# A gated cross-attention and mixture-of-experts layer: bias as one matmul step, half-tile input load, one pair in the prologue, norm root on GpSimd, new step lists

## The reference, cut to what matters

```python
# x (8, 512, 256), ctx (8, 512, 128); 16 heads of 64; 8 experts, top 2
def xattn(q, kv):                       # per batch
    qh, kh, vh = heads(q @ Wq), heads(kv @ Wk), heads(kv @ Wv)
    attn = softmax(qh @ kh.T * 64 ** -0.5)
    return merge(attn @ vh) @ Wo + bo
def ffn(x):
    probs = softmax(x @ gate_w.T)
    comb = one_hot_weights(top_k(probs, 2))          # (tokens, 8)
    return sum(comb[:, e:e+1] * (x @ expert_w[e].T + expert_b[e]) for e in range(8))
x = x + tanh(g_xattn) * xattn(layernorm(x), ctx)
x = x + tanh(g_ffn) * ffn(layernorm(x))
```

## Time and profile before

| | |
|---|---|
| median of 3 runs | 1139.79 us (1138.34 to 1140.05) |
| profiled execution | 1140.45 us, span of its instructions 1138.6 us |
| mean granted TensorE clock | 0.975 |
| TensorE matmul busy | 1056.2 us (93%) |
| VectorE | 881.0 us (77%) |
| ScalarE | 812.9 us (71%) |
| GpSimd | 602.7 us (53%) |

### The profile page before, as it was taken

One profiled execution on the slowest core, in us unless ns is written; L12 is line 12 of the kernel. 1 busy time (PEld: TensorE's weight loads), 2 busy tenths in 40 slices (PEclk: granted clock), 3 DMA queues, 4 the chain that ended last, 5 costly groups with the idle time before them and its releaser, 6 DMA issues.

```text
span 1138.6 us, 29422 instructions
## 1 busy us (share of the span) xinstructions
PE 1056.2 (93%) x10784; PEld 786.4 (69%) x10784; DVE 881.0 (77%) x1559; ACT 812.9 (71%) x1403; POOL 602.7 (53%) x323
## 2 busy tenths in 40 slices
PE   8877898999989999899898999899998999999878
PEld 7555676677667776677676777667776777667676
DVE  7786688877887779877588778877788777887537
ACT  4878887678867698586695878667895768858500
POOL 2655665464645656465464756446565555647400
PEclk9889999999999999999899999999998999999999
DMA  3996968496685876676766868739676678669610
GB/s 126 192 181 131 175 150 143 90 177 129 135 134 116 158 155 123 123 148 120 136 135 127 159 121 168 140 84 177 131 135 140 117 140 158 125 109 162 123 33 18
DMA packets 554209, 152.09 MB, mean 134 GB/s; under 512 B 541896, under 2 KB 551504, under 8 KB 554064
## 3 DMA queue, kind: packets, MB, share of 16 engines
q1 hardware_dynamic: 554064, 150.16, 67.8%
HBM read 11.68 MB, written 4.19 MB: 14 GB/s over the span
## 4 chain that ended last, share of the span: by engine, by line
PE 64%; issue 12%; DVE 9%; POOL 8%; ACT 4%; DMA 2%; SPq 1%; DVEq 0%; POOLq 0%; ACTq 0%
PE MB L963 32%; PE ST L1070 14%; PE PV L1086 10%; POOL p_s L488 7%; PE MB L973 3%; PE ST L1095 2%; DMA pt_s<-p_s 2%; ACT pf L628 1%; PE ST L963 1%; PE MB L1043 1%; DVE p L925 1%; DVE nmax L787 1%; DVE ve L688 1%; DVE w L903 1%; DVE stats L676 1%
## 5 line engine op out<-in xcount | busy, mean ns | idle before, releaser
L488 POOL TENSOR_TENSOR p_s<-pf,p_s 128x1024 f16<-128x1024 f32 x256 | 549.7, 2147 | 456.9 <-ACT p_s L637 456.2
L787 DVE TENSOR_REDUCE nmax<-ST 128x2 f32<-128x1024 f32 x256 | 311.3, 1218 | 70.0 <-PE ST L1070 66.0
L628 ACT ACTIVATE pf<-ST,shifts 128x512 f32<-128x512 f32 x512 | 323.3, 686 | 3.2
L1086 PEld LDWEIGHTS PV<-v_s,pt_s 128*128 128x128 f16 x6144 | 206.3, 98 | 111.9 <-issue 71.5
L637 ACT ACTIVATE p_s<-pf 128x1024 f16<-128x1024 f32 x256 | 270.6, 1057 | 7.2
L1086 PE MATMUL PV<-v_s,pt_s 128*128 128x65 f16 x6144 | 233.1, 195 | 43.2 <-DVE o_n L803 35.5
L963 PE MATMUL MB<-ex_s,x2t_s 128*128 128x512 f32 x708 | 201.8, 422 | 0.0
L619 ACT ACTIVATE shifts<-nmax 128x2 f32<-128x2 f32 x256 | 51.7, 202 | 162.7 <-DVE nmax L787 162.0
L750 DVE SCALAR_TENSOR_TENSOR acc<-MB,comb,acc 128x256 f32<-128x256 f32 x236 | 114.1, 484 | 61.5 <-PE MB L963 56.7
L963 PEld LDWEIGHTS MB<-ex_s,x2t_s 128*128 128x128 f32 x708 | 129.6, 196 | 40.8 <-issue 16.5
L1070 PE MATMUL ST<-KH,QH 64*128 64x512 f32 x512 | 129.5, 502 | 19.5 <-ACT pf L628 12.2
(11 more groups left out here) (120 smaller groups left out, 1119.9 us busy)
## 6 DMA issues: line engine op xcount, KB each, us to landing
pt_s<-p_s SPq DMA_TRANSPOSE x512, 2.8
xin<-x SPq DMA_DIRECT2D x8, 512.0 KB, 4.7
out<-acc SPq DMA_DIRECT2D x8, 512.0 KB, 4.5
kvin<-kv_t SPq DMA_DIRECT2D x8, 256.0 KB, 4.2
acc<-expert_t SPq DMA_DIRECT2D x4, 256.0 KB, 3.9
xn<-expert_t SPq DMA_DIRECT2D x4, 256.0 KB, 4.3
pf<-wq SPq DMA_DIRECT2D x1, 768.0 KB, 7.1
pt_s<-wk SPq DMA_DIRECT2D x1, 512.0 KB, 5.7
```

The source lines that it names most:

```text
L488: pool.tensor_tensor(p_s[:, u, 1, :, :], pf[:, u % 2, :, :], p_s[:, u, 0, :, :], ALU.subtract).then_inc(p_lo, 1)
L628: last = act.activation(pf[:, u % 2, i, :], ST[u % 2][:, i, :], ACT.Exp, bias=shifts[:, u % 2, i:i + 1], scale=SCALE)
L787: dve.tensor_reduce(nmax[:, t % 2, :], ST[t % 2][:, :, :], AX.X, ALU.max, negate=True)\
L1086: last = pe.matmul(PV[:, col:col + HEAD + 1], pt_s[:, slot, a, i, k, :], v_s[:, c, k, (2 * p + i) % HEADS, :], start=(k == 0 and n == 0), ...
```

## The change

One diff with these edits:

- The bias of the experts: expert_b stands three times in a 72-row operand (`eb_s`: high part in rows 0 to 7 and 64 to 71, low part in 32 to 39, the rest zero), comb in 72 columns (high part at 0 and 32, low at 64), and each bias job becomes two fp32r matmuls of 256 columns. comb is written by one instruction, its copy into two places and its low part by two more; the gates job transposes 72 columns.
- x of batch 0 is loaded in two halves, and its sums start with the first.
- The prologue does q and k of one pair; q1, k1 and the bound come behind the first score tile of the first batch (PRO_JOBS).
- var + eps, the power, mean times it and its negative are four GpSimd instructions; lines 687 and 688 are gone. In the prologue GpSimd holds its own work back until xn is written; there and in the epilogue TensorE transposes each tile of xn as it comes.
- The logits are reduced and shifted straight from the bank; route part 0 is gone.
- The output of the last batch is stored in four DMAs, one for each tile.
- p_s has three slots, used as a ring, instead of four. Values stand six units back instead of five.
- The dummies ahead of ("x2t", 0) in the epilogue are put ahead of whichever x2t job comes first (NEXT_X2T); in the new order that is x2t0.
- Late weights use other rows and slots.
- All four step lists are replaced.

```diff
-PE_ORDER = (
...
+PE_ORDER = (
+    "scores", "scores values v2,0 v0,0 v1,0", "scores values v3,0", "scores values ot6 values", "scores k2 k3 values",
+    "scores values q2 ot7", "scores values", "scores values v3,1 wo3,0 v0,1", "scores values", "scores wo3,1 q3",
+    "scores values", "scores v2,1 ot0 values", "scores values q4 values x2t0 x2t1 k4", "scores values router v1,1",
+    "scores values logits k5 values", "scores ot1 k6 values", "scores values q6 wo0,1", "scores values",
+    "scores values q5 wo0,0", "scores values", "scores values q7 k7 expert0,0",
+    "scores values expert0,1 ot3 expert0,2 ot2 expert0,3 values", "scores",
+    "scores values expert1,0 bound wo1,1 expert1,1", "scores expert1,2 gates expert1,3 wo1,0 values",
+    "scores expert2,0 xt1 expert2,1 values", "scores values expert2,2 xt0",
+    "scores values expert2,3 ot4 expert3,0 bias0 values", "scores",
+    "scores bias1 expert3,1 ot5 q0 expert3,2 k0 wo2,1 q1 k1", "scores", "scores values expert3,3 wo2,0 values",
+)
-ACT_ORDER = (
...
+ACT_ORDER = (
+    "shift exp hi copy", "shift hi exp hi", "shift copy exp hi hi", "shift copy exp hi copy", "shift hi exp",
+    "shift copy exp hi copy hi", "shift exp hi copy", "shift exp hi copy", "shift exp", "shift copy exp hi copy",
+    "shift exp hi copy norm2 hi", "shift", "shift hi exp hi hi copy exp hi", "shift copy hi exp logits hi copy",
...
-DVE_ORDER = (
-    "maximum normalise take take", "maximum take take", "maximum normalise take", "maximum take normalise",
-    "maximum take take", "maximum take take take take sums2", "maximum moments2 take normalise", "maximum",
-    "maximum take take normalise bound", "maximum take normalise take take take take", "maximum take take normalise",
-    "maximum take route0 take route1", "maximum route2 take route3 take route4 take route5 normalise route6 take",
...
+DVE_ORDER = (
+    "maximum", "maximum take", "maximum normalise take take", "maximum take normalise take", "maximum take",
+    "maximum normalise", "maximum take take take normalise", "maximum take take", "maximum take",
+    "maximum take sums2", "maximum moments2 normalise take", "maximum take", "maximum normalise take take take take",
+    "maximum normalise take take sums1 take take", "maximum normalise route1 take", "maximum take moments1",
+    "maximum route2 take normalise route3", "maximum take", "maximum normalise route4 take take",
+    "maximum route5 take route6", "maximum normalise bound take take take", "maximum take take take take normalise",
...
-VALUES_BACK, SHIFT_BACK, EXP_BACK, COPY_BACK = 5, 0, 0, 0
+VALUES_BACK, SHIFT_BACK, EXP_BACK, COPY_BACK = 6, 0, 0, 0
-PF_SLOTS, P_SLOTS, PT_SLOTS = 2, TT, 6
+PF_SLOTS, P_SLOTS, PT_SLOTS = 2, 3, 6
-LATE_SLOTS, LATE_HI_AT, LATE_LO_AT = 4, 3, 4
+LATE_AT = list(range(10)) + [13, 14]
+LATE_SLOT = [0, 1, 2, 3, 0, 1, 2, 3, 0, 1, 0, 1]
+LATE_IN_XN = 8
+PRO_JOBS = 4
+NEXT_X2T = [name for name in LAST_JOBS if name[0] == "x2t"][0]
+BUSY_EPI = {("ot", PAIRS - 1): 3, ("wo", ROUNDS - 1, 0): 6, NEXT_X2T: 24, ("router",): 5, ("logits",): 3}
...
-            sp.dma_start(xin[:, :, :], x_v[:, 0:TT, :]).then_inc(x_in, 16)
+            sp.dma_start(xin[:, 0:2, :], x_v[:, 0:2, :]).then_inc(x_half, 16)
+            sp.dma_start(xin[:, 2:TT, :], x_v[:, 2:TT, :]).then_inc(x_in, 16)
...
+            sp.wait_ge(const_pool, 1)
+            for row0 in (0, 32, 64):
+                sp.dma_start(eb[row0:row0 + EXPERTS, :], expert_b).then_inc(small_in, 16)
...
+            for t in range(TT):
+                sp.wait_ge(job_free, epi.last_done(JOBS, ("bias", t // 2), ("expert", t, EC - 1)) + BANKS)
+                sp.dma_start(out_v[:, (BATCHES - 1) * TT + t:(BATCHES - 1) * TT + t + 1, :],
+                             acc[:, t:t + 1, :]).then_inc(y_out, 16)
...
+            pool.memset(eb[:, :], 0.0).then_inc(const_pool, 1)
             pool.memset(ident[:, :], 0.0).then_inc(const_pool, 1)
+            pool.memset(comb_w[:, :, :], 0.0).then_inc(const_pool, 1)
...
                 pool.wait_ge(var, n)
+                pool.tensor_tensor(ve[:, :], mv[:, :, 1], eps[:, :], ALU.add).then_inc(rstd_done, 1)
+                pool.wait_ge(rstd_done, 3 * n - 2)
                 pool.tensor_tensor(rstd[:, :], ve[:, :], minus_half[:, :], ALU.pow).then_inc(rstd_done, 1)
-                pool.wait_ge(rstd_done, n)
-                pool.tensor_tensor(shift[:, :], less[:, :], rstd[:, :], ALU.mult).then_inc(shift_done, 1)
+                pool.wait_ge(rstd_done, 3 * n - 1)
+                pool.tensor_tensor(shift[:, :], mv[:, :, 0], rstd[:, :], ALU.mult).then_inc(rstd_done, 1)
+                pool.wait_ge(rstd_done, 3 * n)
+                pool.tensor_tensor(shift[:, :], zero[:, :], shift[:, :], ALU.subtract).then_inc(shift_done, 1)
 
             power(1, ln1_var, ln1_rstd, ln1_shift)
+            pool.wait_ge(ln1_done, 1)
...
-                if it.kind != FIRST or p > 0:
-                    act.wait_ge(hi_turned[u], 16 * pair_count(it.b, p - 1))
-                act.activation(p_s[:, u, 0, :, :], pf[:, u % 2, :, :], ACT.Copy).then_inc(p_hi, 1)
+                before = divmod(p * TT + u - P_SLOTS, TT)
+                if it.kind != FIRST or before[0] >= 0:
+                    act.wait_ge(hi_turned[before[1]], 16 * pair_count(it.b, before[0]))
+                act.activation(p_s[:, it.ring(p, u, P_SLOTS), 0, :, :], pf[:, u % 2, :, :], ACT.Copy).then_inc(p_hi, 1)
...
-                    last = dve.tensor_copy(m1[:, :, :], m[:, 0:TT * EXPERTS].rearrange("p (t e) -> p t e", t=TT))
+                    raw = m[:, 0:TT * EXPERTS].rearrange("p (t e) -> p t e", t=TT)
+                    dve.tensor_reduce(less[:, :], raw, AX.X, ALU.max, negate=True).then_inc(lg_max, 1)
+                    dve.wait_ge(lg_max, it.b)
+                    last = dve.tensor_tensor(logit[:, :, :], raw, over(less), ALU.add)
...
-                    dve.tensor_scalar(comb[:, :, :], m2[:, :, :], tg[:, 1:2], None, ALU.mult).then_inc(comb_ready, 1)
+                    then(dve.tensor_scalar(comb[:, :, :], m2[:, :, :], tg[:, 1:2], None, ALU.mult))
+                    twice = comb_w[:, :, 0:64].rearrange("p t (a e) -> p t a e", a=2)[:, :, :, 0:EXPERTS]
+                    then(dve.tensor_copy(twice.bitcast(F32R),
+                                         comb[:, :, :].unsqueeze(2).broadcast_to([P, TT, 2, EXPERTS])))
+                    dve.tensor_tensor(comb_w[:, :, 64:WIDE].bitcast(F32R), comb[:, :, :], comb_w[:, :, 0:EXPERTS],
+                                      ALU.subtract).then_inc(comb_ready, 1)
...
+                    dve.tensor_tensor(eb_s[32:32 + EXPERTS, :], eb[32:32 + EXPERTS, :],
+                                      eb_s[32:32 + EXPERTS, :].bitcast(F32), ALU.subtract).then_inc(const_dve, 1)
...
-                        last = pe.matmul(m[:, DIM * i:DIM * (i + 1)], comb_t[:, tile(2 * name[1] + i)],
-                                         eb[:, :], start=True, stop=True)
+                        last = pe.matmul(m[:, DIM * i:DIM * (i + 1)], gates_t[:, tile(2 * name[1] + i)],
+                                         eb_s[:, :], start=True, stop=True)
```

More of the change, by code:

```diff
@@ L65 @@
 PE_ORDER = (
[L66 to L71, removed]
@@ L98 @@
+    "maximum take take take take take", "maximum take", "maximum take take take normalise",
 )
 POOL_ORDER = (
-    "low", "low", "low", "low", "low residual", "low power2", "low", "low", "low", "low", "low", "low", "low",
-    "low power1", "low", "low", "low", "low", "low", "low", "low", "low", "low", "low", "low", "low", "low",
-    "low context", "low", "low", "low", "low",
+    "low", "low", "low", "low", "low", "low", "low", "low", "low power2", "low residual", "low", "low", "low", "low",
@@ L320, in build @@
         small_in = sem("small_in")
-        late_in = [sem(f"late_in{n}") for n in range(LATE_SLOTS)]
+        late_in = [sem(f"late_in{n}") for n in range(4)]
         w_hi, wq_lo, w_lo = sem("w_hi"), sem("wq_lo"), sem("w_lo")
@@ L599, in row @@
                             exponential(b, *divmod(at, TT))
+                        if kind == FIRST and at == 0:
+                            for name in HI[PRO][PRO_JOBS:]:
+                                take_hi(pro, name)
                     elif part == "copy":
@@ L854, in row @@
                             maximum(b, *divmod(at, TT))
+                        if kind == FIRST and at == 0:
+                            for name in JOBS[PRO][PRO_JOBS:]:
+                                take_first(name)
                     elif part == "normalise":
@@ L910, in first @@
                     then(dve.tensor_tensor(mask[:, :, :], w1[:, :, :], over(r1), ALU.is_equal))
-                if part == 0:
-                    dve.wait_ge(job_free, it.done(JOBS, ("logits",)) + BANKS)
-                    then(dve.tensor_reduce(r1[:, :], m1[:, :, :], AX.X, ALU.max, negate=True))
-                    dve.tensor_tensor(logit[:, :, :], m1[:, :, :], over(r1), ALU.add).then_inc(lg_shift, 1)
-                elif part == 1:
```

(14 more changed lines are left out.)

188 lines of the change are left out of this document (98 added, 90 removed).

## The result

| | before | after |
|---|---|---|
| median, same chip | 1139.07 us (4 runs, 1134.05 to 1140.05) | 1059.43 us (4 runs, 1055.02 to 1060.98) |
| ratio | | 0.9303, 95% interval 0.9263 to 0.9343 |
| profiled execution, span | 1140.45, 1138.6 us | 1055.02, 1053.2 us |
| mean granted TensorE clock | 0.975 | 0.994 |

Faster, as forecast, but by 80 us instead of 35: the forecast of 1104.5 is 45 us too high and its range (1085 to 1124) doesn't hold the result. Rows of a profile are of one execution; the changed kernel's is the quickest of its four, so spans in the rows differ by 85 us.

A forecast was written before the change was run, and what follows sets the result against it. TensorE was taken to set the length of a batch. From 1140.45 us, 25.2 (3.6 in each of seven batches), 9.1 (epilogue) and 1.0 (first batch) gave 1105.15, or 1104.5 against the median; range 1085 to 1124.

The forecast's parts named there:

- Net I take 2.0 us of waiting off each batch, bounds 4.9 (all gone, nothing new) and -1: New step lists: o_n waits of 4.9 us per batch shrink, some new waiting comes, 2.0 us net gain.
- 1 to 3 us at row 19 for held route steps: VectorE's worst new row, 4.6 to 6.6 us of work against TensorE's 1.7: 1 to 3 us of o_n wait may stay.
- 1 to 2 for ScalarE's rows 0 to 10: New rows 0 to 10: ScalarE needs 36 us beside TensorE's 31, so 1 to 2 us of new waiting stay.
- First batch: Late weights move to rows 13 and 14, the norm waits for 8 of 12: 1 us less, bounds -4 and +4.
- Prologue: Transposes come 0.7 us later behind dummies, first maximum earlier as q1, k1 and bound move: 0, bounds -1.5 and +1.5.
- The dummies: Epilogue: 48 dummy instructions fill TensorE's idle time for xn, so the router begins 6.8 us earlier, bounds 5.5 to 7.2.
- The epilogue: After the last batch: dummies 6.8, bias 1.4 and smaller last store 0.9 us less, sum 9.1.
- The root on GpSimd: Norm: lines 687 and 688 leave VectorE, GpSimd gets small instructions of 0.2 us each and has room: nothing.
- All o_n waits vanish: Rival, batches with experts: new waits are 0.4 us at most, 42.7 us gained, so 1087 us; chance 0.20.
- The waits only move: Rival: held copy, comb and ScalarE's rows eat row 12's gain; bias and epilogue remain, 1119.5 us; chance 0.22.
- Slower by the ring of three: Rival: p_s copies wait for transposes that wait for values; at 4 us more per batch 1147 us; chance 0.08.
- the likeliest case: The forecast itself, 1104.5 us with its own range 1096 to 1113, new waits at row 19 and ScalarE included; chance 0.50.

The follow-up runs named there:

- experiment 4: Kernel before, with 16 dummy matmuls put into TensorE's wait for o_n ahead of values unit 10 of each batch but the first: 1126.47 us, ratio 0.9924.
- experiment 8: Changed kernel with route parts 1 to 6 packed into row 16 of VectorE's list, ahead of its normalise: 1105.8 us, ratio 0.9723.
- experiment 10: Changed kernel with the four old lists, but row 12's normalise on VectorE after route part 3 instead of part 5: 1088.22 us, ratio 0.9533.
- experiment 5: Changed kernel with its bias jobs as plain float32 matmuls over the same 72 rows, instead of fp32r: 1073.28 us, ratio 0.9445.
- experiment 6: Kernel before, with only the 24 dummies of the epilogue put ahead of x2t1, which its order has first: 1130.4 us, ratio 0.9945.
- experiment 2: Changed kernel with the root's two small steps (old lines 687 and 688) back on VectorE: 1058.2 us, ratio 0.9332.
- experiment 9: Changed kernel with the four old lists and the root's two small steps back on VectorE: 1113.38 us, ratio 0.9765.

## Why the prediction was wrong in size

**The step that failed** is "Net I take 2.0 us of waiting off each batch, bounds 4.9 (all gone, nothing new) and -1", together with what the sum of a batch left out. The direction was right, and that waiting for o_n goes. The waiting was sized too small, and two terms were missing: the clock behind the waits, and the time of TensorE's products in the new order. The seven batches with experts, first maximum of batch 1 to the last maximum (windows as rows 1, before and after):

```profile
143.10:1071.60 928.50, 886.15 (x9177) 652.47 (x9177) 744.49 (x1312) 694.62 (x1201) 515.00 (x262) 0.98 0.71 136
...
134.60:994.40 859.80, 844.69 (x9145) 649.08 (x9146) 720.37 (x1293) 678.24 (x1202) 522.78 (x288) 1.00 0.88 147
```

| seven batches, us | before | after | change | per batch | forecast per batch |
|---|---|---|---|---|---|
| idle | 42.4 | 15.1 | -27.2 | -3.9 | -2.0 |
| lost at the lower clock (half of the busy time at 0.50) | 13.6 | 1.7 | -11.9 | -1.7 | 0 |
| bias jobs | 14.8 | 4.1 | -10.7 | -1.5 | -1.6 |
| all other work, at full clock | 857.8 | 838.9 | -18.9 | -2.7 | 0 |

For the second line TensorE was busy for 27.2 us at the clock of 0.50 before, and for 3.4 after. Within batch 2, from the start of each product to the start of the next, less idle time:

| batch 2, us | before | after |
|---|---|---|
| idle | 6.14 | 0.79 |
| expert jobs | 25.98 | 23.56 |
| scores | 29.59 | 28.92 |
| values | 24.48 | 25.10 |
| bias jobs | 2.11 | 0.57 |
| q jobs | 12.35 | 11.78 |

- *Waiting that I left in.* I kept 1 to 3 us at row 19 for held route steps and 1 to 2 for ScalarE's rows 0 to 10. Measured in batch 2 are 0.6 us for o_n and 0.2 for pf. Over the seven batches the waits for pf are 2.8 us, 0.4 each. Both sums were too large. Row 19 took VectorE 3.4 us in batch 2 and 5.5 in batch 3, where I had 4.6 to 6.6: its seven small steps are 0.2 us each. ScalarE's 36 us beside 31 of TensorE took off only about 2 us for the overlap of its instructions; at 0.1 for each of its 62 instructions it is 6. In batch 2 their durations in these rows add up to 37.0 us, and ScalarE is busy for 30.87 of 31.93 (the window's fourth pair), TensorE for 31.89:

```profile
258.73:290.66 31.93, 31.89 (x379) 23.46 (x376) 26.92 (x46) 30.87 (x56) 22.87 (x13) 1.00 1.13 194
```

- *The clock after a wait was not in the sum of a batch at all.* It is in experiment 4 (7 to 9 us of the run with the wait left in place) and experiment 8. The bound of 4.9 was the idle time of the two waits, and the true price of the large one was, in five of seven batches, that plus 1.7 to 3.1 us lost at half clock. For the earlier trace rows this could have been read beforehand: a window over the 5 us behind 333.98.
- *Products closer together.* In batch 2 idle -5.35, bias -1.54 and the one slow expert job (-1.2, 2.70 to 1.49) make 8.1 of 11.7. Scores, q and the other expert jobs lost another 2.4 us together with the same number of products, values gained 0.6, and the rest is in k, wo and transposes. The clock is not the cause: in the kernel before it is 1.00 in all of batch 2 but 334.6 to 338.0 (the windows at experiment 4), after it is 1.00 throughout. One thing that differs is what a job stands next to. Of the 24 q and expert jobs of batch 2, 13 stood directly ahead of a score tile in the old order, and 12 of these took 1.57 to 1.60 us from start to start, like the one of 1.57 in the earlier trace rows; the six ahead of values took 1.49 to 1.51. In the new order 3 stand there, and none of the 24 takes over 1.51, those 3 included:

```profile
340.36 1.55 PE L1021 MATMUL MB<-ex_s,x2t_s 128*128 128x512 f32 x6
341.84 0.50 PE L1131 MATMUL ST<-KH,QH 64*128 64x512 f32 x2
```

  In experiment 10, with the old order of TensorE, batch 2 is 127.0 us at clock 1.00, 124.66 of it busy against 121.48. So this part comes with the order of the whole and not with the routing. Why a job in front of a score tile was slow, the runs don't show.
- *First batch.* Forecast -1.0, bounds -4 and +4, measured -6.3. With old lists it is 120.7, with new ones 113.9 to 115.0: the lists, outside my bounds. The clock is in it again: some 20 us at 0.50 before (mean 0.91), some 10 after (0.96), worth 5.1 us. TensorE also idles 4.0 us less, and has 2.8 us more work there at full clock. Which rows of the lists do it was not tried.
- *Prologue.* Forecast 0, measured -2.2 (bounds ±1.5). The transposes came 0.2 us later (forecast 0.7), since the 72 dummies took 9.97 us and not 10.43; but only one pair stands between them and the first score tile.

**What was right.** The bias: 12.8 over 16 jobs forecast; from start to start they are 12.2 shorter (the two of batch 2 last 0.57 us, those of the epilogue 0.46), and 14 to 16 by experiment 5, new waits included. The dummies: 6.8 forecast, 6.7 in the profile, 6.3 by experiment 6. The epilogue: 9.1 forecast, 8.2 measured. The root on GpSimd: nothing, and nothing it is (experiment 2). Three slots of p_s: no new waits of TensorE for transposes (0.5 us in all, 6.3 before), and ScalarE's copies waited for them three times, 1.9 us in all. The place in the lists: row 12 of VectorE, half of their gain by experiment 10.

**The rivals.** "All o_n waits vanish" (1087, chance 0.20) is what came nearest, and it too lacks the clock and the products; 9.3 us are left of the waits. "The waits only move" is out by the 26.2 us. "Slower by the ring of three" is out by the rows on transposes. I gave the likeliest case 0.50 with two new waits that only list arithmetic spoke for; the old trace had no row of either.

## What to carry to other kernels

The price of a wait on TensorE can be the wait plus a slow stretch behind it, and it was so for five of seven here: look at the granted clock of the few microseconds after each long one before you bound what its removal can give. Small steps of another engine cost by where they stand: ask of each what the next instruction behind it releases, and spread them behind the release, not ahead of it. A one-word move in the old list was worth 21 us, and packing one row of the new one cost 48, with the same work. And before you set the rows of one engine against those of another, take the overlap of its instructions off each of them: here 0.1 us on some 60 of them was most of a debt of 5 us that wasn't there.

## What the runs showed of the hardware that was not expected

- A wait of 3.5 us of TensorE in batch 2 was followed by 4.5 us at 0.50 to 0.70 of the clock, and one of 6.2 us had the lower level already within it (0.62 in the window 325 to 328, 0.50 in 328 to 331 of experiment 8). The length of the wait does not decide alone: after 3.12 us in batch 3 the mean was 0.62, after 3.13 us in batch 4 it was 1.00, and in the first batch, full of waits, it was 0.62 after one of 1.42 us (window 115.59 to 120.09). Products of no use in the wait of batch 2 kept the clock at 1.00, and over the run they paid for themselves.
- Whether a small VectorE instruction is held until one of GpSimd's ends goes with where the lists put it, and so batch for batch: the same line 722 took 1.0 to 1.5 us in 8 of 16 with the old lists (experiment 9), and 1.95 us in one and 0.17 in the 15 others with the new (experiment 2).
- The same six matmuls of 512 columns took 1.57 to 1.60 us directly ahead of a score tile (12 of 13) and 1.49 to 1.51 ahead of values, at clock 1.00 in both cases (batch 2 before). In the changed kernel the three ahead of a score tile took 1.47 to 1.48, so what stands behind a job is not all of it.
- Dummies beyond the arrival of the data cost what they last: 17 dummies (34 instructions) fewer in the prologue brought its first maximum 3.5 us forward.
